# Vision tower on one Trainium2 core: weight split, skip product and final waits put elsewhere in their queues

## The reference

```python
h = concat(cls_tok, concat(class_token, patches @ W_lin + b_lin) + pos)
x_mlstm, z = split(layernorm(h) @ W_up)            # 256 -> 2 x 512
x_act = swish(causal_conv4(x_mlstm) + conv_b)
q, k = headwise(x_act, Wq), headwise(x_act, Wk); v = headwise(x_mlstm, Wv)
Dmat = exp(logD - mD)                              # decay from gates, lower triangle
C = (q k^T) * DH**-0.5 * Dmat
hs = (C / (max(|sum C|, exp(-mD)) + 1e-6)) v
h = h + ((head_norm(hs)*norm_w + skip * x_act) * swish(z)) @ W_down
h = h + shared_swiglu(ln(h)) + routed_swiglu(top1 of 32 experts)   # sigmoid score
```

## Time and profile before

| | |
|---|---|
| Median of 3 executions | 687.18 us (686.2 to 687.49) |
| The profiled execution | 689.14 us |
| Its span, first to last instruction | 687.4 us |
| Mean granted TensorE clock | 0.977 of full speed |
| PE, DVE, ACT, POOL busy | 92%, 68%, 57%, 33% |
| Last of the three loads that ACT's split waits for (`chan_t`) | issued at 4.03 us, 6.5 us to landing |
| ACT's first table load, ahead of its first copy | from 13.24 us, 1.28 us long |

### The profile page before, as it was taken

The page is one execution under the profiler, slowest core; times in us unless marked ns, Lnnn a source line. Parts: engine busy times, 40 slices in busy tenths (PEclk is TensorE's granted clock), DMA queues, the critical chain, the costliest instruction groups (busy, mean ns, idle before and its releaser), DMA issues.

```text
span 687.4 us, 11733 instructions
## 1 busy us (share of the span) xinstructions
PE 634.0 (92%) x4029; PEld 535.2 (78%) x4029; DVE 467.2 (68%) x1528; ACT 391.5 (57%) x863; POOL 230.0 (33%) x249
## 2 busy tenths in 40 slices
PE   5899899999999999999999999888899999999994
PEld 3688778868968967977977988756688888888883
DVE  1644795876776786786686885858577767667761
ACT  0428558529628627636745938514466666666661
POOL 4000210144044054054044241554336666421551
PEclk9999899999999999999999989999999999999998
DMA  8239210030030030022011010155699999999960
GB/s 289 113 92 366 89 53 1 18 92 20 6 103 20 1 99 28 2 54 70 4 32 35 10 33 12 40 181 182 238 410 376 377 381 383 355 303 406 397 225 22
DMA packets 46258, 101.65 MB, mean 148 GB/s; under 512 B 10951, under 2 KB 32245, under 8 KB 41328
## 3 DMA queue, kind: packets, MB, share of 16 engines
q1 hardware_dynamic: 35184, 89.07, 35.9%
q0 software_dynamic: 9488, 8.52, 4.6%
q10 hardware_dynamic: 1520, 3.23, 1.5%
HBM read 80.17 MB, written 23.32 MB: 151 GB/s over the span
## 4 chain that ended last, share of the span: by engine, by line
PE 63%; DVE 16%; ACT 11%; issue 4%; POOL 3%; DMA 3%; SPq 0%; POOLq 0%; DVEq 0%
PE bank L2227 16%; PE bank L1354 10%; PE bank L2246 9%; PE bank L1476 4%; PE bank L1322 4%; DVE stats_h L950 3%; PE bank L1455 3%; PE bank L1418 2%; PE bank L2235 2%; PE bank L1380 2%; PE bank L1331 2%; POOL rstd_h L433 2%; ACT cw L571 2%; ACT hst L552 2%; DVE mv_h L953 2%
## 5 line engine op out<-in xcount | busy, mean ns | idle before, releaser
L433 POOL TENSOR_TENSOR rstd_h<-var_h,minus_half 76x4 f32<-76x4 f32 x32 | 32.3, 1010 | 181.3 <-DVE var_h L964 181.3
L2045 POOL DMA_INDIRECT out<-rows,bg x32 | 37.9, 1185 | 68.0 <-DVE rows L2117 61.1
L2227 PE MATMUL bank<-w_hi,x_hi 128*128 128x512 f32 x148 | 56.5, 463 | 2.9 <-DVE x_lo L2129 2.9
L1322 PE MATMUL bank<-patch,lin_w 128*128 128x288 f32 x192 | 51.3, 420 | 8.3 <-DMA col_t<-cols 7.9
L1322 PEld LDWEIGHTS bank<-patch,lin_w 128*128 128x128 f32 x192 | 36.5, 196 | 19.8 <-issue 10.6
L867 DVE SCALAR_TENSOR_TENSOR y<-xm,conv_t,y 128x296 f32<-128x296 f32 (+2 forms) x96 | 43.7, 510 | 10.1 <-ACT xm L483 10.1
L1816 POOL DMA_INDIRECT x_zone_dram<-xs_rows,spot x32 | 40.2, 1256 | 23.5 <-ACT xs_rows L604 11.4
L1816 POOL DMA_INDIRECT b_zone_dram<-base_rows,spot x32 | 37.7, 1179 | 26.9 <-DVE base_rows L1079 18.4
L2227 PE MATMUL bank<-w_lo,x_hi 128*128 128x512 f32 x148 | 46.3, 394 | 0.0
L2153 DVE TENSOR_TENSOR act_e<-silu_e,bank 128x512 f32<-128x512 f32 x37 | 25.5, 688 | 30.5 <-PE bank L2227 30.5
L2227 PE MATMUL bank<-w_hi,x_lo 128*128 128x512 f32 x148 | 46.1, 393 | 0.0
(11 more groups left out here) (254 smaller groups left out, 1776.8 us busy)
## 6 DMA issues: line engine op xcount, KB each, us to landing
wts<-w_exp SPq DMA_DIRECT2D x18, 1024.0 KB, 12.3
x_act<-w_exp SPq DMA_DIRECT2D x10, 1024.0 KB, 11.0
silu_z<-w_exp SPq DMA_DIRECT2D x9, 1024.0 KB, 11.4
wts_down<-w_exp SPq DMA_DIRECT2D x18, 512.0 KB, 10.2
patch<-patches SPq DMA_DIRECT2D x8, 864.0 KB, 6.5
down_w<-w_exp SPq DMA_DIRECT2D x10, 512.0 KB, 10.2
lin_w<-w_exp SPq DMA_DIRECT2D x9, 512.0 KB, 10.8
b_zone_dram<-act_t SPq DMA_DIRECT2D x1, 4160.0 KB, 28.2
```

Source lines behind the costliest of these rows:

```text
L433: pool.tensor_tensor(rstd_h[:, j, :], var_h[:, j, :], minus_half[:], ALU.pow).then_inc(s_rstdh, 1)
L1322: last = pe.matmul(fb[c][:, 0:GS * N], lin_w[:, k, c * 128:(c + 1) * 128], patch[:, k, :], start=(k == 0), stop=(k == KF - 1))
L2045: pool.indirect_dma_start(out, bass.IndirectOffsetOnAxis(ap=rows_at, axis=0), rows[:, k % 4, :], None, bounds_check=T - 1, oob_is_err=Fals ...
L2227: last = pe.matmul(banks[2 + 2 * e + u][:, :], x[:, e, c * SLOT:(c + 1) * SLOT], w[:, e, u, c * I:(c + 1) * I], start=(n == 0), stop=(n == ...
```

## The change

Five edits, in one diff:

- ACT splits the up weights before it copies the first token rows, not behind them.
- DVE makes the first half of `up_lo` before the statistics of the first group, the second half between these and the normalising, instead of both behind the normalising.
- In the first attention step (`a.n == 0`) ACT's `skip_of` goes from before the last `xm_of` and the exponentials to behind `exp_m_d`. Other steps keep their order.
- PE gets one more filler matmul behind `to_columns` in step 1.
- POOL no longer waits for the landing of its last scatters. Those waits are at the end of SP's queue, the extra slots' under nested `If`s.

```diff
 # ScalarE
             def step(e, f, a, m):
                 if a: q_of(a)
+                if f and f.n == 0: split_up()
                 if f: h_rows_of(f)
-                if f and f.n == 0: split_up()
...
-                if a: skip_of(a)
+                if a and a.n > 0: skip_of(a)
                 if f: xm_of(f, 3)
...
                     exp_m_d(a)
+                    if a.n == 0: skip_of(a)
 # VectorE
-            def split_up():
-                for z in range(2):
-                    half = slice(z * INNER, (z + 1) * INNER)
-                    dve.wait_ge(s_split, z + 1)
-                    dve.tensor_tensor(up_lo[:, :, half], up_raw[:, :, half], up_hi[:, :, half].bitcast(f32),
-                                      ALU.subtract).then_inc(s_prep, 1)
+            def split_up(z):
+                half = slice(z * INNER, (z + 1) * INNER)
+                dve.wait_ge(s_split, z + 1)
+                dve.tensor_tensor(up_lo[:, :, half], up_raw[:, :, half], up_hi[:, :, half].bitcast(f32),
+                                  ALU.subtract).then_inc(s_prep, 1)
...
                 if f:
+                    if f.n == 0: split_up(0)
                     ln1_stats(f)
+                    if f.n == 0: split_up(1)
...
                     xn_of(f)
-                    if f.n == 0: split_up()
 # TensorE
                 if f: to_columns(fb, xn, s_xn, f.n, s_xnt_mm)
+                if f and f.n == 0: stream(ab[3], lin_w, 1)
 # SyncE, end of its queue
+            with ExitStack() as deep:
+                for k in range(E, ALL):
+                    deep.enter_context(sp.If(extra > k - E))
+                    stored(sp, k)
+            for k in range(E - 4, E):
+                stored(sp, k)
 # GpSimd, end of its queue
                     scatter(k, put[:, k - E:k - E + 1].bitcast(u32))
-                    stored(pool, k - 1)
-                    with pool.If(extra < k - E + 2):
-                        stored(pool, k)
-                    pool.nop()
-            for k in range(E - 4, E):
-                stored(pool, k)
```

## The result

The changed kernel took 680.86 us (median of 6 runs, 678.11 to 684.15), the kernel before 687.1 beside it (6 runs, 685.47 to 687.49). The ratio is 0.9916, with a 95% interval of 0.9886 to 0.9945: faster by 6.2 us, where 5.9 was forecast for the sum and 681.3 for the time. Run a second time as an experiment of its own, the same kernel took 679.79 (6 runs), ratio 0.9899 [0.9872, 0.9925]. The profiled execution took 678.11 with a span of 676.3, at a mean granted TensorE clock of 0.993; the one before took 689.14, 687.4 and 0.977. So this pair differs by 11.1 us of span, 5 more than the medians do, and a part of what it shows is not the change. That is the main difficulty in reading it.

A forecast was written before the change was run, and what follows sets the result against it. TensorE is busy 92% of the span, so gains must come where PE waits or runs slowly, or at the ends. Front 2.0, skip 1.5 and end 2.4 sum to 5.9: 687.2 to 681.3 us, range 679.3 to 684.4.

The forecast's parts named there:

- front: Kernel start: earlier weights' split plus full clock at the up product, 2.0 us in all, bounds 0.5 and 2.9.
- skip: Step 2: four skip instructions leave the path ahead of table load and exponentials; 1.5 us, upper end 1.76, lower end nothing.
- end: Kernel end: POOL drains right behind its last scatter while SP waits for the landing; gain 2.4 us, lower bound 0.65.
- the order: Kernel start: splitting up weights earlier starts the up product sooner; 0.6 us with POOL held, 1.46 without any hold.
- POOL is not held: Rival, kernel start: DVE's subtraction and POOL's power run side by side; order gives 1.46, time 680.4 us, chance 0.15.
- The clock at the up product: First up product: shorter PE idle time, with the filler between, keeps full clock; 1.4 us, or nothing if it falls.
- the clock falls anyway: Rival, first up product: transposes too thin to keep the clock; gain 4.5, time 682.7 us, chance 0.22.
- The filler's own price: Behind step 1's transposes: one more matmul takes 0.45 us, lies in PE's idle time and costs nothing.
- the DRAIN waits for the transfer: Rival, kernel end: DRAIN's 2.45 us run only behind the landing; end gains 0.65, time 683.0 us, chance 0.11.
- Eaten later: Rival, later steps: two or more new low-clock stretches, each costing up to 1.67 us, leave 684 to 687; chance 0.09.
- rows waiting for weights: Rival, kernel start: ACT awaits the weights' landing before the rows, one us per us behind 14.8; chance 0.03.
- new stretches at 0.50 after 100 us: Sign against the forecast: granted TensorE clock newly falling to half after 100 us would show it wrong.

The follow-up runs named there:

- skip behind in all steps: Changed kernel with the skip product behind the decay's exponentials in every loop step, not only the first attention step; 682.51 us, ratio 0.9929 to the kernel before.
- end alone: Kernel before with the final landing waits on SP instead of POOL, nothing else; 684.83 us, ratio 0.9964.
- skip alone: Kernel before with the first attention step's skip product moved behind the decay's exponentials, nothing else; 683.74 us, ratio 0.9939.
- before, with the pause: Kernel before, whose POOL fills a tile 16 times (some 5 us) between the last landing and its final DRAIN; 691.46 us, measured once.
- before, with four fillers: Kernel before with four filler matmuls in PE's idle time ahead of the first attention step's heads; 685.84 us, ratio 0.9985.
- order alone, no filler: Kernel before with the up weights split ahead of the rows on ACT and DVE, without the filler matmul; 686.08 us, ratio 0.9986.
- both together: Changed kernel with the second half of the weights' subtraction behind `xn` and one filler matmul ahead of the first heads; 680.3 us, ratio 0.9909.

## Why the prediction was right, point by point

**The sign and the time.** Three places gave 5.6 us by direct reading of the profiled pair, against a forecast of 5.9: front 1.5, skip 1.9, end 2.2. The medians moved by 6.2 (0.9916, so 3.8 to 7.8 us). The 11.1 us of the profiled pair contain some 5.4 more, by ACT's instructions: 1.6 at 106.8, 2.1 at 396.9 and 1.7 at 444.7, where before's execution had stretches at 1.2 GHz and the changed one had not. The last two are not the change. No other profile has one at 444.7, whichever part of the change it contains, and only one of the other eleven (the skip behind in all steps, at 396.1) has one at the place of 396.9. The first is another matter. All five profiles with the old order at the start have a stretch at 103.6 to 107.0, and none of the seven with the new order has one:

| kernel | stretches at 1.2 GHz in the first 120 us, start in us |
|---|---|
| before | 24.9, 35.1, 72.7 (6.8 long), 106.8 |
| end alone | 24.4, 34.7, 72.2 (6.8 long), 106.4 |
| skip alone | 25.0, 35.3, 103.6 |
| before, with the pause | 24.6, 34.8, 72.4 (6.8 long), 106.5 |
| before, with four fillers | 25.1, 35.4, 86.6, 107.0 |
| order alone, no filler | 26.5, 70.9 (13.7 long) |
| changed, no filler | 34.1, 71.6 (10.2 long) |
| changed, skip behind in all steps | 24.1, 34.3, 78.7 |
| changed | 32.0, 76.4 |
| changed, again | 32.0, 76.4 |
| changed, second half behind `xn` | 32.2 |
| both together | 31.4 |

Each of the seven gains 1.6 us on before at that place, though nothing is edited there. So these 1.6 us seem to belong to the change, and the prediction had no term for them; how the order at the start leads to it is not shown. That the sum still came out near is partly luck: by the paragraphs below the order, the clock and the end were put too high by 0.1, 0.2 and 0.5, the skip too low by 0.4, and this term was missing. By the times, the profiled pair's 11.0 us are the medians' 6.2 with 2.0 that before's execution took over its median and 2.75 that the changed one took under its own; the forecast had assumed the 2.0 for both.

**The order, 0.6 forecast.** Right in mechanism, slightly too high. POOL was held as forecast: 1.11 us against 0.23, ending 0.09 after DVE (forecast 0.05 to 0.06). `xn_hi` began at 23.39 (forecast 23.2; the embedding was 0.14 later). The distance in the first table fell by 0.46 us, which is just under the lower bound of 0.5. The term that was too small is the way from the second `xn_hi` to PE: it ended at 24.13 and PE started at 24.85, 0.72 later, where the estimate of 0.45 for one `xn_lo` had made it 0.60. POOL's loss was 0.88 instead of 0.86. The Trainium skill (SBUF — State Buffer, Who interferes with whom) says that a DVE instruction with two SBUF inputs contends with a GpSimd instruction that reads SBUF, since its second input comes through an interface that the two share. The 1.11 against 0.23, ended 0.09 us behind DVE's subtraction, agrees, and the kernel with the half behind `xn` shows the other side, 0.23 again. The rival "POOL is not held" fell by that. When it was made true by moving the half, it was worth 0.67 more, not 0.86, as the subtraction then stands ahead of `xn_lo`.

**The clock at the up product, 1.4 forecast.** Kept in this execution (1.00). The lead by step 2 is 1.52 us; with 0.14 for the later embedding and without the 0.46 of the order, the clock gave 1.2. Reckoned in the same way it is 1.2 in the changed kernel run again, and 1.4 in the kernel without the filler, the one with the half behind `xn`, the one with both, and even the order alone, whose clock fell midway through the product. What these six have in common is in the table above: one stretch at 1.2 GHz before 40 us, where the old order has two. The changed order, held or not, kept the clock through this product in five of seven profiles; the old order lost it there in all five. So the rival "the clock falls anyway", priced at 0.22, is what two of seven executions did, one of them (the skip behind in all steps) with two stretches before 40 us as in the old order. With the clock goes the idle time of PE before the product, 2.58 us before and 0.33 to 1.23 in the six. Together with that before the transposes it is 3.00 us before, 2.54 with the order and no filler, 1.64 in the changed kernel and 0.96 with the half behind `xn`, and at 2.54 the clock fell in the product in one execution and not in the other. So it isn't shown which idle time keeps it. That the filler does it isn't supported here, since the clock stayed without it and fell at 24.1 with it. Seven executions can't settle the filler's share, and it stays open.

**The filler's own price.** Mis-sized: I divided 3.60 us by 8 records, but the 8 records were 4 calls. One call leaves two records and takes 1.07 us, not 0.45. It still fitted: PE had 0.33 us to spare.

**The skip, 1.5 forecast.** Right in mechanism, too low in size: 1.54 us at the table load in the profiled pair and in the kernel that has this part alone (from 0.08 behind to 1.46 ahead), but 1.9 in both by 86.74, over the upper end of 1.76. What the term left out is DVE's wait for the slow heads, 0.35 us; the prediction has the heads in no sum. The table load behind the skip came at 74.08 in that kernel, against a forecast of 74.1. The cover that I named, ACT's wait of 3.95 us before the second `silu_z`, was itself a product of the slow heads: with the heads at full clock it is gone, ACT goes from load to `silu_z` without a gap, and PE waits for it instead, in the changed kernel:

```profile
74.24 0.30 PE L1408 MATMUL bank<-g_w,xn_hi 128*76 128x16 f32 x2 [1.05 <-ACT silu_z L522]
```

That wait takes back part of the 2.5 us that the faster heads win for PE. Of these 2.5 the path gets only the 0.35, as DVE's norms and statistics are the chain behind the heads. The net gain of the part doesn't suffer from the wait.

**The end, 2.4 forecast.** Measured 2.2 on the profiled pair and 2.5 in the medians of the part alone. But 0.3 of the 2.2 is a landing that came 3.0 us after the scatter's start instead of 3.3. From the landing (the branch past it) to the drain's end it was 3.1 us before and is 1.2 now, so the move gives 1.9; by the span's end behind the scatter's start, the mean is 6.83 in four profiles with the old end (6.64 to 7.06; the one with the pause aside) and 4.89 in seven with the new. The step that failed is who arrives last. I had the DRAIN run its 2.45 us beside the transfer and SP as the last to arrive. In fact SP had drained at 675.32 and POOL's drain ended at 676.07; it waits for the transfer, with 1.22 to 1.23 us behind the branch in the three traces shown. The prediction had named the sign against it, a DRAIN record that reaches past the landing, and that sign came: 3971 ns. The rival "the DRAIN waits for the transfer" was right in mechanism and wrong in price: it put all 2.45 us behind the landing and a gain of 0.65, but only 1.2 us are left behind the landing. The term came out near by luck: 2.45 us running beside the transfer and then 0.9 of SP's way is not far from a drain with 1.2 left.

**Eaten later, and rows waiting for weights.** Neither came in the changed kernel's profiles: ACT's copies ran from 14.45 without a wait for the load, and the rows were copied from 16.96, where PE was the last to be ready. As for new stretches at 0.50 after 100 us, the changed kernel's profile has none until PE is idle at the end.

## What to carry to other kernels

Work that an engine does on data which doesn't depend on what it waits for belongs into the wait; but ask what the neighbour reads meanwhile, since a DVE instruction with two SBUF inputs lengthened a POOL operation of 0.23 us to 1.11 and took back more than half of what the order had to give (0.67 of 1.13). An instruction moved off the path can also change the clock of what follows: 0.35 us of the skip's 1.9 came from heads that no longer ran at 1.2 GHz. A price that is read as a group's time over its count is only right if a call leaves one record. A gain of 1% at a clock that moves by itself is read from distances within a trace and from medians of many runs, not from the spans of one pair of profiles; and before a stretch at low clock is put down to chance, it is looked up in all profiles with and without the change.

## What the runs showed of the hardware

- POOL's closing DRAIN, after indirect DMAs, took 2450 ns when it began behind the landing (in five profiles, 0.7 us behind it and once 6.6), and 3971, 3983 and 5096 ns when it began under the transfer, each time ending 1.22 to 1.23 us behind SP's branch past the landing; SP's own took 13 ns.
- The landing of the same last scatter came 3.0 us after its start in one execution of the changed kernel and 4.1 in another.
- A POOL operation on 76x4 values, begun 0.17 us after a DVE subtraction of two SBUF tensors, took 1.11 us instead of 0.23 and ended with it, in each of the five profiles with that order for which the table gives it.
- The granted clock falls to 0.50 at different places in executions of nearly the same code (396.9 and 444.7 in one, none there in the end alone), but not only by chance: a stretch near 106 us is in all five profiles with the old order at the start and in none of the seven with the new. The mean over the span went from 0.977 to 0.995 in the profiles shown.
- Heads that ran at 1.2 GHz took 6.21 us instead of 3.72, and of these 2.5 us the path had 0.35.
